# Scores beside values, and both row normalisations of a step on GpSimd

## What is computed

```python
def attn(x, mu_k, mu_v, mu_r, Wk, Wv, Wr, W_out, w, u):      # RWKV time mixing over axis 0
    k = (mu_k * x + (1 - mu_k) * x_prev) @ Wk.T              # v and r alike: three "mixes"
    num, den = conv(exp(k) * v), conv(exp(k))                # decayed sums: the state
    return (sigmoid(r) * num / den) @ W_out.T
def xattn(query, ctx):                                       # 16 heads of width 16
    p = softmax(clip(q @ k.T * scale, -1e4, 1e4))
    return (p @ v) @ Wo + bo
def ffn(x):                                                  # 16 experts, 4 per token, 2 shared
    return routed_experts(x) + shared_expert(x)
x = layernorm(x + attn(x, ...))
x = layernorm(x + xattn(x, ctx))
x = layernorm(x + ffn(x))
```

## Time and profile before

| | us |
|---|---|
| runs (3), median | 1068.57 (1068.05 to 1074.94) |
| profiled execution, its own time | 1061.99 |
| span of its instructions | 1060.2 |
| PE busy | 968.2 (91%) |
| DVE busy | 772.2 (73%) |
| ACT busy | 687.2 (65%) |
| POOL busy | 594.0 (56%) |

### The profile page before, as it was taken

One profiled execution on the slowest core, in us unless ns is written; L12 is line 12 of the kernel. 1 busy time (PEld: TensorE's weight loads), 2 busy tenths in 40 slices (PEclk: granted clock), 3 DMA queues, 4 the chain that ended last, 5 costly groups with the idle time before them and its releaser, 6 DMA issues.

```text
span 1060.2 us, 21641 instructions
## 1 busy us (share of the span) xinstructions
PE 968.2 (91%) x6502; PEld 750.1 (71%) x6502; DVE 772.2 (73%) x1666; ACT 687.2 (65%) x2182; POOL 594.0 (56%) x651
## 2 busy tenths in 40 slices
PE   4678999999999999989999999888799999999896
PEld 2456667777777677667776776667688888887775
DVE  3477999999999999999999999763432222465687
ACT  1168777767868777766777777774446556666533
POOL 4552464766756746747467473222545555666654
PEclk8789999999999999998999999999999999999998
DMA  9804334433343331113111110113345544788765
GB/s 256 247 19 147 97 118 160 133 127 130 131 162 129 117 121 60 49 53 119 47 60 50 60 43 28 63 58 106 125 121 155 153 143 123 247 258 259 233 216 182
DMA packets 97872, 135.38 MB, mean 128 GB/s; under 512 B 11203, under 2 KB 83554, under 8 KB 97761
## 3 DMA queue, kind: packets, MB, share of 16 engines
q1 hardware_dynamic: 84704, 101.53, 31.7%
q0 software_dynamic: 13056, 32.47, 8.3%
HBM read 61.91 MB, written 76.23 MB: 130 GB/s over the span
## 4 chain that ended last, share of the span: by engine, by line
PE 64%; DVE 13%; POOL 8%; issue 8%; ACT 4%; another core or an unknown queue 1%; DMA 1%; SPq 1%; DVEq 0%; POOLq 0%; ACTq 0%
PE bU L580 8%; PE bT L594 7%; PE four L849 6%; PE four L775 6%; PE four L890 5%; PE bT L849 5%; PE bM L713 5%; DVE Sc L1337 4%; PE bO L811 4%; POOL mix L1673 3%; PE bM L580 3%; PE bM L740 3%; POOL mix L1671 2%; DVE wkv L1314 2%; POOL rstd L1653 1%
## 5 line engine op out<-in xcount | busy, mean ns | idle before, releaser
L1070 ACT ACTIVATE Sc<-Sc,nmx 128x256 f32<-128x256 f32 x512 | 253.6, 500 | 5.1 <-DVE nmx L1339 5.1
L1078 ACT ACTIVATE PT<-bT 128x512 f32<-128x512 f32 x256 | 151.7, 593 | 142.4 <-PE bT L594 141.0
L1733 POOL DMA_INDIRECT Yt<-PT,dests x150 | 150.1, 1001 | 108.9 <-issue 56.4
L1337 DVE TENSOR_SCALAR Sc<-four 128x1024 f32<-128x1024 f32 x128 | 156.1, 1220 | 36.3 <-PE four L775 29.7
L594 PE MATMUL bT<-idn,Sc 128*128 128x128 f32 x1024 | 163.4, 283 | 6.6 <-ACT PT L1078 5.6
L594 PEld LDWEIGHTS bT<-idn,Sc 128*128 128x128 f32 x1024 | 115.6, 142 | 73.2 <-issue 60.6
L1339 DVE TENSOR_REDUCE nmx<-Sc 128x4 f32<-128x1024 f32 x128 | 156.2, 1220 | 4.4
L1716 POOL DMA_INDIRECT Xs<-x,slots x120 | 120.1, 1001 | 35.2 <-issue 18.6
L1070 ACT ACTIVATION_READ_ACCUMULATOR Sc<-Sc,nmx 128x1 f32 x512 | 99.0, 193 | 0.0
L775 PE MATMUL four<-KT,QT 32*128 32x256 f32 x1024 | 76.3, 408 | 12.8 <-DVE Sc L1337 9.0
L1449 DVE SCALAR_TENSOR_TENSOR tgb<-tgb,four 128x256 f32<-128x256 f32 x47 | 19.7, 420 | 90.4 <-ACT tgb L1123 85.1
(11 more groups left out here) (229 smaller groups left out, 2004.6 us busy)
## 6 DMA issues: line engine op xcount, KB each, us to landing
Xs<-yg SPq DMA_DIRECT2D x16, 1768.0 KB, 8.2
xb<-Xs SPq DMA_DIRECT2D x152, 136.0 KB
yg<-Yt SPq DMA_DIRECT2D x27, 512.0 KB
W<-w SPq DMA_DIRECT2D x4, 1152.0 KB, 11.3
xTs<-xT SPq DMA_DIRECT2D x16, 256.0 KB
x<-x SPq DMA_DIRECT2D x16, 256.0 KB
Base<-stg SPq DMA_DIRECT2D x15, 256.0 KB
out<-acc SPq DMA_DIRECT2D x15, 256.0 KB
```

The lines of the kernel that those rows point to most:

```text
L1070: last = fn(Sc[:, n % 3, m, t, :], Sc[:, n % 3, m, t, :], ACT.Exp, bias=nmx[:, n % 3, m, t:t + 1], accum_out=rs[:, s % 2, t, h:h + 1])
L1078: fn(flat(PT[:, h % RING]), bT[:, :], ACT.Copy).then_inc(a_pt.sem, 1)
L1337: ts(Sc[:, n % 3].rearrange("p m t k -> p (m t k)"), flat(score_banks(n)), CLAMP, -CLAMP, ALU.min, ALU.max).then_inc(d_clip.sem, 1)
L1733: pool.indirect_dma_start(Yt, bass.IndirectOffsetOnAxis(ap=dests[:, i % IDS, b:b + 1], axis=0), y_rows(i)[:, b, :], None, bounds_check=SPA ...
```

## The change

On PE, scores now come behind the first transposition of a slot, with values right behind them; `Wo` moves ahead of both in slot 2; `t_chunk` 5 moves behind the second transposition; `t_chunk` 8 moves ahead of 7. ACT copies `rT` before `ao` in slot 0. DVE loses both normalisations, writes the negated means instead, does `x2` and its moments ahead of the clip of slot 2, takes plan part 0 ahead of `invert`, plan part 1 in slot 4 instead of 1, and `shared_sum` ahead of the router's last part. GpSimd applies the normalisations behind each root, and its third mix moves behind `state`. The last step's `x2` is treated alike in the tail.

```diff
-PLAN_AT = {0: 0, 1: 1, 7: 2}
+PLAN_AT = {0: 0, 4: 1, 7: 2}
@@ PE, slot(s, g) @@
-                if 0 <= n + 2 < PAIRS:
-                    scores(n + 2)
                 if A and g == 3:
                     context_k(a, 0)
+                if T and g == 2:
+                    t_chunk(t, 2)
                 if heads:
                     turn_probs(n, 0)
+                if 0 <= n + 2 < PAIRS:
+                    scores(n + 2)
+                if g % 2 == 0 and 0 <= n - 2 < PAIRS:
+                    values(n // 2 - 1)
...
-                if T and g == 5:
-                    t_chunk(t, 5)
...
-                if g % 2 == 0 and 0 <= n - 2 < PAIRS:
-                    values(n // 2 - 1)
-                if T and g == 0:
-                    t_chunk(t, 0)
                 if heads:
                     turn_probs(n, 1)
...
+                if T and g == 5:
+                    t_chunk(t, 5)
                 if T and g == 6:
                     t_chunk(t, 6)
                 if T and g == 7:
+                    t_chunk(t, 8)
                     t_chunk(t, 7)
-                    t_chunk(t, 8)
@@ ACT, slot(s, g) @@
                 if T and g == 0:
+                    t_chunk(t, 0)
                     copy_out(t)
-                    t_chunk(t, 0)
@@ DVE, moments(n, s, src) @@
+                if n < 2:
+                    ts(mean[:, n, :], mv[:, n, :, 0], -1.0, None, ALU.mult)
                 ts(vpe[:, n, :], mv[:, n, :, 1], EPS, None, ALU.add).then_inc(d_vpe[n].sem, 1)
@@ DVE, slot(s, g) @@
-                if T and g == 3:
-                    norm(1, t, x2[:, t % 2, :, 0:D], x2[:, t % 2, :, 0:D], d_x2)
+                if T and g == 2:
+                    t_chunk(t, 2)
+                    dve.wait_ge(d_z2.sem, d_z2.at(t))
+                    moments(1, t, x2[:, t % 2, :, 0:D])
                 if 0 <= n + 2 < PAIRS:
                     clip(n + 2)
+                if s in PLANS and g in PLAN_AT:
+                    plan(PLANS[s], PLAN_AT[g])
                 if A and g == 0:
                     invert(a, 1)
                     finish_wkv(a)
...
-                if A and g == 2:
-                    norm(0, a, x1, x1, d_x1)
@@ GpSimd @@
+            def norm(n, s, rows, done):
+                rsqrt(n, s)
+                pool.wait_ge(g_rstd[n].sem, g_rstd[n].at(s))
+                for t in range(NT):
+                    last = pool.tensor_scalar(rows[:, t, :], rows[:, t, :], mean[:, n, t:t + 1], rstd[:, n, t:t + 1], ALU.add, ALU.mult)
+                last.then_inc(done.sem, 1)
...
                 if B:
-                    mixes(b)
+                    mixes(b, 0)
                 pairs(1)
                 pairs(2)
-                if A:
-                    rsqrt(0, a)
-                if T:
-                    rsqrt(1, t)
+                roots(s)
                 send(s - 2, 1)
                 pairs(3)
                 if A and a + 1 < L:
                     state(a)
+                if B:
+                    mixes(b, 1)
```

## The result

Over 20 runs of each kernel the median goes from 1065.61 us to 1075.96 us; the ratio is 1.0082 (95% interval 1.0063 to 1.0102). The change makes the kernel slower by 0.8%, where a gain of 4 us was forecast. It is within the 1% called no change, yet clear of noise, and of the other sign. The base of the forecast, 1068.57, was the median of three runs and 3 us above that of the twenty.

What follows compares the result with a forecast made beforehand. PE (91% busy) bounds the kernel, DVE nearly as full, at most 1.5 us a step of idle time to win. 8.8 - 10.5 - 3.5 + 1 = -4.2 us, giving 1064 from a 1068.57 median; 8-in-10 range 1048 to 1076.

Steps and rivals of the forecast that it cites:

- first steps: Steps -1 and 0: shorter wait, faster query projection, and 4 counted in step 0; -10.5 us (6 to 12).
- step 10: Plan's first number comes right behind the clip, so the 3.39 wait and low clock go; -3.5 us (1.5 to 5).
- tail: Two TENSOR_SCALAR stand ahead of sends and scatters on GpSimd's queue; +1 us (0.7 to 1.5); steps 14, 15 nothing.
- the waits vanish: Rival: PE is the bound, idle time and entries won in 11 steps; 1036, halfway 1050 to 1057; chance 0.25.
- the change does nothing to the steps: Rival: only the first steps and step 10 gain; -13, 1055 us; chance 0.13.
- +0.8 a step: Steps 2 to 9 and 11 to 13: a step ends at 42.3 against 41.5; +8.8 us over 11 steps.
- Slot 4, slot 6: Leading transpositions wait for ACT's copies: slot 4 starts at 19.6 (before 19.0), slot 6 at 30.7 (scores before 29.6).
- Scores beside values: PE: one entry into narrow matmuls, 0.09, saved per pair of blocks; bounds nothing or twice this.
- `Wo` moved ahead: PE, slot 2: ao comes at 10.2, so PE waits 1.3 us where it waited nothing, with later work queued behind.
- `rT` ahead of `ao` is worth nothing: ACT, slot 0: no gain, as PE gets to Wo earlier and waits there.
- The lock: Rival: GpSimd locks DVE's new means, x2 and slot 2's clip 1.25 later; +11, 1075 us; chance 0.17.
- GpSimd: Third mix leaves, 2.3 us; four TENSOR_SCALAR of 128x256 come at 0.5 each, 2.0; x2 ready about when it was.

Runs made afterwards that it cites:

- first pair: the profiled executions of the kernel before and the change; spans 1060.2 and 1075.3 us.
- second pair: both kernels traced once more without an edit on one chip; steps 2 to 9 take 332.6 us before and 342.0 with the change.
- sv_back: the change with scores back at the slot's head and values back ahead of the second transposition; ratio to the kernel before 0.9952.
- sv_only: the kernel before with only scores moved behind a slot's first transposition and values right behind them; ratio 1.0202.
- change_start: the change with scores at the slot's head and values in their old place in steps up to 1 only; ratio to the kernel before 1.0010.
- wo_back: the change with Wo back behind transposition, scores and values in slot 2, and DVE's x2 back behind the clip; ratio to the kernel before 1.0199.
- sv_rt: sv_back with ACT copying ao ahead of rT and PE's transposition of rr back behind values; ratio to the kernel before 0.9858.
- best_dve: best with both normalisations back on DVE and the three mixes together; ratio to the kernel before 1.0540.
- norms_only: the kernel before with GpSimd's part alone (both normalisations, negated means, third mix behind state), all other orders as before; ratio 1.0113.
- the four kernels after sv_back: sv_back with slot 5's shared expert, slot 7's order, or ACT's copies with rr's transposition put back, or all three; ratios 0.9900, 0.9928, 0.9858, 0.9924.
- each half alone: the kernel before with GpSimd's part alone, ratio 1.0113, or with the orders on PE, ACT, DVE and the plan alone, ratio 1.0104.
- the faster order: best, run again with GpSimd's sum of the numerators waiting for DVE's rr; ratio to the kernel before 0.9842, against 0.9950 without the wait.
- best: sv_rt with the shared expert of slot 5 also back ahead of the second transposition; ratio to the kernel before 0.9888, on another chip 0.9950.

## Why the prediction was wrong, point by point

The terms of the sum against both pairs of traces, in us (the 11 like steps are the stretch from the `add_x` of step 2 to that of step 14, less step 10):

| term | forecast | first pair | second pair |
|---|---|---|---|
| up to the first `add_x` | 0 | +3.4 | -2.3 |
| first steps | -10.5 | -6.4 | -9.2 |
| 11 like steps | +8.8 | +13.9 | +13.6 |
| step 10 | -3.5 | -2.6 | -3.9 |
| tail | +1 | +6.7 | +6.6 |
| sum | -4.2 | +15.1 | +4.7 |

The first row moves both ways and is noise. Three terms were mis-sized, all too kindly to the change: the tail by 5.6, the like steps by 5, the first steps by 1 to 4. A sum of two large terms of opposite sign leaves a small one, and these misses turned it. That the order at the slot heads is the main cost is shown by sv_back, sv_only and change_start; the tail is open in part. Of the rivals, *the waits vanish* (steps 2 to 9 below 330) and *the change does nothing to the steps* fell with the 341.7 of steps 2 to 9.

- **+0.8 a step, under-sized: 1.2 to 1.3.** 42.55 measured for 42.3, against 41.4 and not 41.5 in a plain step of the kernel before, and 42.9 to 43.0 where `pack` was locked. The likeliest case went to 1.2.
- ***Slot 4, slot 6*, right.** 19.81 for a forecast 19.6, 30.93 for 30.7, from the holds of ACT that the sum was built on. That the holds cost is shown by sv_back.
- ***Scores beside values*, no saving to be seen.** 0.09 a pair was forecast. sv_only, which has nothing else, leaves PE's busy time where it was (320.29 for 320.16); the change as a whole has 1.7 less in eight steps. The Trainium skill (TensorEngine Tiling (Array Packing), Key Properties) says that a change of tiling mode drains the array, and by that the saving could be nil, as sv_only has it.
- ***`Wo` moved ahead*, right in mechanism and size, wrong in sign.** PE starts it 10.29 after the leading transposition (358.10 - 347.81), forecast 10.2. It waits 0.78 and not 1.3, as the wait in slot 1 took the rest. But I costed the move by itself and called it a loss. wo_back shows that without it the step is 0.6 longer: GpSimd's chain for `x2` needs it.
- ***`rT` ahead of `ao` is worth nothing*, right in the change.** The wait moved from the product with `rT` (0.23) to the next transposition (0.47), but PE waits for `ao` behind it anyway. With scores at the head again the wait is 0.38 to 0.55 and no other stands behind it. What it costs there is not shown, as sv_rt undid two moves at once.
- ***The lock*, right in mechanism, and the victim depends on the order.** In the change `mean` and `vpe` go by in 0.19 and 0.15 in a steady step, while `sum_num` locks out `pack`. In sv_back it is `mean` (1.26), as the rival had it; in best_dve `vpe` (1.27) and the norms; in norms_only and the four kernels after sv_back `pack` and `taken`.
- ***GpSimd*.** 0.55 an instruction for a forecast 0.5; `x2` is in time in the change. I had no price for leaving the norms on DVE. It is up to 2.65 more for four instructions where they meet sends and state (best_dve, 4.02 for 1.37).
- ***First steps*, over-sized.** The parts of step -1 came: the wait at `x1` fell by 4.1 and the projection by 1.8. In step 0 I counted 4 of gain and let the transposition at the head wait for ACT at no price. The transpositions at two heads wait 1.79 and 2.17; with scores there instead the stretch falls from 112.4 and 110.7 to 105.6 (change_start), 5 to 7 more than the change won. I had also called a wait of 2.0 well short of one with a slow clock behind it. Behind the 1.79 the granted clock was 0.58 from 70 to 74 us, and the scores took 2.09; behind the 2.17 it was 1.00.
- ***Step 10*, -3.5, right.** -2.6 and -3.9; 45.59 for a forecast 44.7, with a clock of 1.00.
- ***Tail*, +1, the largest miss.** "Steps 14, 15: nothing" was wrong: the waits at the heads and in front of the shared expert (1.8 for 1.2) are longer as other work runs out, 2.1 to 2.8 more ahead of the first unit. The rest of the +6.6 and +6.7 is not explained.

## What to carry to other kernels

In an order written by hand, an instruction that waits for the engine behind it should not stand at the head: put there a block that needs nothing new (here the scores), above all in the first steps. Price a move together with the moves that depend on it, since here each half alone lost 1.0 to 1.1% and one piece of the change lost 2.0% by itself. Where two engines lock each other out, start the long operation by a semaphore that says that the short ones are done. It gained 1.3% in the faster order, where much was held, and nothing that the ratio shows in the change.

## What the hardware showed

- Running GpSimd instructions held a DVE operation of 128x8 for up to 1.69 (0.16 alone), and four of 128x256 for 4.02 (1.37 in another order). The Trainium skill (SBUF — State Buffer, Who interferes with whom) tells of this lock; the runs add its price, 1.3 us in eight steps of one order and 7.0 in another.
- A DVE operation that is held can stay so through several GpSimd instructions in a row. The `pack` of 1.69 started at 297.76, during a send (297.36, 0.97), and ended at 299.45, 0.04 behind the sum's first instruction (298.36, 1.05), which followed the send by 0.03. The norm of 2.84 in best_dve outlasted a send and two instructions of the state.
- The lock depends on phase: the same kernel (best) had `pack` at 0.16, 0.36, 0.23, 0.38, 1.24, 1.00 in six steps in a row in one execution and 0.97, 0.73, 0.16, 0.67, 1.28, 1.17 in another, on another chip, and steps 2 to 9 at 333.0 and 336.4.
- GpSimd's TENSOR_SCALAR of 128x256 with two column operands takes 0.55.
- The tail of one kernel took 395.7 on one chip and 413.5 on another, while its first steps took 105.1 on both.
